# Joining the feature halves of chosen couples on Vector, Silu on Scalar, and expert rows stored by their tile's code

## The reference

```python
# part 2: shared expert and 8 routed experts, the best two per position
shared = silu(x @ Wg_s.T) * (x @ Wu_s.T) @ Wd_s.T
for e in range(8):
    out = out + cw[..., e:e+1] * (silu(x @ Wg[e].T) * (x @ Wu[e].T) @ Wd[e].T)
# part 3: every position against each of 64 text rows
txt_proj = einsum('btd,de->bte', textual, Ws)
feat_proj = einsum('bfd,de->bfe', features, W)
h = tanh(txt_proj[:, None] + feat_proj[:, :, None] + b)     # 512 x 64 x 256 per batch
rho = einsum('bftd,d->bft', h, w[:, 0])
att = softmax(rho + mask)
# part 4: activations scaled, rounded and clipped to +-127, times ternary weights
```

## Time and profile before

| what | us |
|---|---|
| median of 3 runs | 1075.21 (1074.61 to 1077.98) |
| the profiled execution | 1065.32 |
| its span, first to last instruction | 1063.6 |

### The profile page before, as it was taken

One profiled execution on the slowest core, in us unless ns is written; L12 is line 12 of the kernel. 1 busy time (PEld: TensorE's weight loads), 2 busy tenths in 40 slices (PEclk: granted clock), 3 DMA queues, 4 the chain that ended last, 5 costly groups with the idle time before them and its releaser, 6 DMA issues.

```text
span 1063.6 us, 23310 instructions
## 1 busy us (share of the span) xinstructions
PE 975.6 (92%) x8716; PEld 768.0 (72%) x8716; DVE 743.3 (70%) x2077; ACT 655.1 (62%) x900; POOL 216.1 (20%) x260
## 2 busy tenths in 40 slices
PE   5889999999899999999999999999999999966752
PEld 2568888888789999877777777777777777623331
DVE  2757767776634356867577578789578578897996
ACT  1211111211011101799999999899999999899991
POOL 1033312333411122211221221221221121210000
PEclk9869989999899999999999999999999999988986
DMA  8012110111179999766565665664764664100000
GB/s 262 26 65 65 65 40 26 45 40 41 59 252 317 337 344 350 273 222 208 178 212 184 212 221 175 220 222 149 239 223 159 236 215 160 49 21 21 2 21 20
DMA packets 114052, 164.20 MB, mean 154 GB/s; under 512 B 13235, under 2 KB 70068, under 8 KB 113940
## 3 DMA queue, kind: packets, MB, share of 16 engines
q1 hardware_dynamic: 104004, 135.57, 38.3%
q0 software_dynamic: 9936, 27.15, 6.9%
HBM read 138.69 MB, written 23.99 MB: 153 GB/s over the span
## 4 chain that ended last, share of the span: by engine, by line
PE 82%; DVE 8%; issue 6%; POOL 1%; DMA 1%; ACT 1%; SPq 0%; POOLq 0%; DVEq 0%
PE bank L1154 24%; PE bank L1336 18%; PE bank L1315 11%; PE bank L1159 11%; PE bank L1306 5%; PE bank L1323 3%; PE bank L1196 2%; PE bank L1140 2%; PE bank L1268 1%; PE bank L1241 1%; PE bank L1209 1%; PE bank L1229 1%; POOL rows_by_expert L563 1%; DVE arena L1009 1%; PE bank L1362 1%
## 5 line engine op out<-in xcount | busy, mean ns | idle before, releaser
L1154 PEld LDWEIGHTS bank<-rowsT,expert_w 128*128 128x128 f32 x2272 | 269.3, 192 | 21.6 <-issue 17.8
L1154 PE MATMUL bank<-rowsT,expert_w 128*128 128x128 f32 x2272 | 281.1, 277 | 0.5 <-DVE rowsT L955 0.5
L653 ACT ACTIVATE act<-bank 128x512 f32<-128x512 f32 x103 | 60.8, 591 | 204.7 <-PE bank L1154 118.5
L578 POOL DMA_DIRECT2D expert_rows<-rows_out x71 | 42.0, 591 | 455.5 <-DVE rows_out L972 455.5
L1315 PE MATMUL bank<-expert_w,act 128*128 128x256 f32 x568 | 134.5, 380 | 0.0
L1159 PE MATMUL bank<-normT,shared_w 128*128 128x256 f32 x512 | 132.7, 410 | 0.0
L1159 PEld LDWEIGHTS bank<-normT,shared_w 128*128 128x128 f32 x512 | 103.0, 208 | 17.0 <-issue 2.6
L669 ACT ACTIVATE tanhs<-shared_w,txtT 128x512 f32<-128x512 f32 x152 | 108.7, 715 | 4.1 <-DVE shared_w L998 4.1
L1315 PEld LDWEIGHTS bank<-expert_w,act 128*128 128x128 f32 x568 | 102.5, 190 | 11.4 <-issue 0.4
L972 DVE COPY rows_out<-bank 128x256 f32<-128x256 f32 x71 | 30.1, 424 | 112.5 <-PE bank L1315 112.4
L670 ACT ACTIVATE tanhs<-shared_w,txtT 128x512 f32<-128x512 f32 x152 | 108.7, 715 | 0.0
(11 more groups left out here) (233 smaller groups left out, 1467.4 us busy)
## 6 DMA issues: line engine op xcount, KB each, us to landing
expert_w<-in_WgT SPq DMA_DIRECT2D x71, 512.0 KB, 4.2
expert_w<-in_WuT SPq DMA_DIRECT2D x71, 512.0 KB, 5.3
expert_w<-in_WdT SPq DMA_DIRECT2D x71, 512.0 KB, 7.1
rows_in<-rows_by_expert SPq DMA_DIRECT2D x71, 128.0 KB, 5.8
expert_rows<-rows_out POOLq DMA_DIRECT2D x71, 128.0 KB, 4.4
x<-in_x SPq DMA_DIRECT2D x8, 512.0 KB, 4.7
out<-x SPq DMA_DIRECT2D x16, 256.0 KB, 2.2
score<-in_fside SPq DMA_DIRECT2D x8, 128.0 KB, 2.2
```

The source lines that it names most:

```text
L653: e.activation(act[n % 2][:, :], banks[2 * (n % 2)][:, :], ACT.Tanh, scale=0.5).then_inc(s_tanh, 1)
L1154: got = e.matmul(bank[:, i * P:(i + 1) * P], w[:, at:at + P], t[:, c * P:(c + 1) * P], start=c == 0, stop=c == DC - 1)
```

## The change

1. **Couple by couple.** The order in a batch is now couple after couple, both halves of each; a buffer holds a couple. `PAIRS` counts couples out of 32 (it counted groups of two couples out of 16): before 14, 8, 8, 14, 8, 8, 20, 26 couples were pre-added in batches 0 to 7 (106), now 24, 18, 15, 18, 12, 14, 20, 27 (148). Both halves' features are copied at a batch's start.
2. **Join.** For the couples of `JOINS` (16, 5, 12, 6, 17, 12, 1, 0 in batches 0 to 7, 69 in all) one DVE instruction on 128x1024 adds half 0 times `ratio` (the quotient of the two weights of w that meet in a lane) to half 1. PE then sums half 1 alone: 4 products in place of 8. PE waits for the join.
3. **Larger and swap.** So that the quotient is at most 1 in size, each feature of half 0 is exchanged with its partner of half 1 where its weight is the larger: 4 DVE instructions, one product, and 25 more DVE instructions (12 of them 128x256) at the start of the program. The text projection waits for them and comes later on all engines, and so does the conversion.
4. **Silu on ACT** for the 71 routed tiles, with one DVE product after it in place of two instructions. The shared expert keeps the old form. The batches' softmax exp is (1+t)/(1-t) with t = tanh(x/2) in batches 0 to 5 (three more DVE instructions on 128x256 each), and stays Exp in 6 and 7.
5. **Tile's code.** A tile's result is stored in DRAM at its code (POOL reads the code first), and the gather uses the slot numbers of the scatter. The search is gone. `expert_rows` grows to 33792 rows of 1 KB (34.6 MB), and ACT issues one transfer, "blank", that fills it with zeros, in its list after the value copies of the prologue. The first store waits for it.
6. **Rounding** in two DVE instructions in place of four.
7. `AHEAD` is 21: the mix stage starts one tile earlier. The other places and lags are set anew (their tables are shown cut).

```diff
--- before.py
+++ after.py
-AHEAD = 22
+AHEAD = 21
...
-PLACES = {"opened": 25.5, "attend": 72, "route": 36.5, "late": -59, "gather_first": -68, "norm_first": -28, "gather": -1, "norm": 42.5,
-          "mix_in_end": -3, "feature": 20, "sum": 5, "preadd": 3, "mix_out": 9, "mix_out_end": 50}
...
-PAIRS = {0: 7, 1: 4, 2: 4, 3: 7, 4: 4, 5: 4, 6: 10, 7: 13}
+PLACES = {"blank": -62, "opened": 25.5, "attend": 72, "route": 36.5, "late": -59, "gather_first": -68, "norm_first": -15.5,
+          "gather": -2, "norm": 42.5, "mix_in_end": -1, "join": 4.5, "sum": 5, "preadd": 5, "mix_out": 9, "mix_out_end": 50}
...
+PAIRS = {0: 24, 1: 18, 2: 15, 3: 18, 4: 12, 5: 14, 6: 20, 7: 27}
+JOINS = {0: 16, 1: 5, 2: 12, 3: 6, 4: 17, 5: 12, 6: 1, 7: 0}
...
-        pairs, share = self.T // 4, int(PAIRS[b])
-        return m // 2 * share // pairs != (m // 2 + 1) * share // pairs
+        pairs, share = self.T // 2, int(PAIRS[b])
+        return m * share // pairs != (m + 1) * share // pairs
...
+    def joined(self, b, m):
+
+        pairs, share = self.T // 2, int(JOINS[b])
+        return (pairs - 1 - m) * share // pairs != (pairs - m) * share // pairs
...
-        late = [[("text", 0)], [("text", 1)], [("spread",)], [("convert",)]]
+        late = [[("larger",)], [("swap",)], [("text", 0)], [("text", 1)], [("spread",)], [("convert",)]]
...
-        outs_dram = nc.dram_tensor("expert_rows", (RT * P, D), F32, kind="Internal").ap()
+        outs_dram = nc.dram_tensor("expert_rows", ((ABSENT + 8) * P, D), F32, kind="Internal").ap()
...
+                    if r == 0:
+                        e.wait_ge(s_tiles, 1)
+                        e.wait_ge(s_blank, 16)
+                    tile = e.value_load(tile_at[0:1, r:r + 1], min_val=0, max_val=ABSENT + 7)
                     e.wait_ge(s_row_bank, row_no["narrow", n] + 1)
-                    e.dma_start(outs_dram[r * P:(r + 1) * P, :], rows_out[r % OUTS][:, :]).then_inc(s_stored[r % OUTS], 16)
+                    e.dma_start(outs_dram[bass.ds(tile * P, P), :], rows_out[r % OUTS][:, :]).then_inc(s_stored[r % OUTS], 16)
...
+                        out=picked[u % PICKED][:, :], out_offset=None, in_=outs_dram,
+                        in_offset=bass.IndirectOffsetOnAxis(ap=slot_of[j % 2][:, i:i + 1], axis=0)).then_inc(s_picked[u % PICKED], 16)
...
+                elif name == "blank":
+                    e.wait_ge(s_zeros, 1)
+                    e.dma_start(outs_dram.rearrange("(p n k) d -> p n (k d)", p=P, n=BLANKS),
+                                zeros.unsqueeze(1).to_broadcast([P, BLANKS, 1024])).then_inc(s_blank, 16)
...
-                    e.activation(act[n % 2][:, :], banks[2 * (n % 2)][:, :], ACT.Tanh, scale=0.5).then_inc(s_tanh, 1)
+                    if is_routed(n):
+                        e.activation(act[n % 2][:, :], banks[2 * (n % 2)][:, :], ACT.Silu).then_inc(s_tanh, 1)
+                    else:
+                        e.activation(act[n % 2][:, :], banks[2 * (n % 2)][:, :], ACT.Tanh, scale=0.5).then_inc(s_tanh, 1)
...
-                        if m % 2:
-                            e.wait_ge(s_wide_in, wide_in_no[u] + 1)
-                            e.activation(wide_pair[u % WIDE // 2], wide_pair[u % WIDE // 2], ACT.Tanh).then_inc(s_wide, 2)
+                        e.wait_ge(s_wide_in, wide_in_no[b, DC - 1, m] + 1)
+                        e.activation(wide_pair[q % PAIR], wide_pair[q % PAIR], ACT.Tanh).then_inc(s_wide, 1)
...
-                        e.activation(w[:, 0:S], featT[ec], ACT.Tanh, bias=txtT[:, ec, t:t + 1])
-                        e.activation(w[:, S:2 * S], featT[ec], ACT.Tanh, bias=txtT[:, ec, t + 1:t + 2]).then_inc(s_wide, 1)
+                        for ec in range(DC):
+                            for j in range(2):
+                                got = e.activation(tiles[ec][:, S * j:S * (j + 1)], featT[ec], ACT.Tanh, bias=txtT[:, ec, t + j:t + j + 1])
+                        got.then_inc(s_wide, 1)
...
-                    e.activation(rho_e[:, :, :], rho[:, :, :], ACT.Exp).then_inc(s_rho_e, 1)
+                    if b < B - 2:
+                        e.activation(rho_e[:, :, :], rho[:, :, :], ACT.Tanh, scale=0.5).then_inc(s_rho_e, 1)
+                    else:
+                        e.activation(rho_e[:, :, :], rho[:, :, :], ACT.Exp).then_inc(s_rho_e, 1)
...
+                    link(e.tensor_scalar(col_abs, cols[:, WW:WW + DC], -1.0, None, ALU.mult))
+                    chain(lambda: e.tensor_tensor(col_abs, col_abs, cols[:, WW:WW + DC], ALU.max))
+                    chain(lambda: e.tensor_tensor(col_larger, col_abs[:, 0:1], col_abs[:, 1:2], ALU.is_gt))
+                    linked(lambda: e.tensor_scalar(larger_diag, ident[:, :], col_larger, None, ALU.mult)).then_inc(s_larger, 1)
...
+                    e.tensor_copy(larger, bank[:, 0:P]).then_inc(done, 1)
+                    e.wait_ge(s_misc[misc["larger",][0]], misc["larger",][1])
+                    by_col = larger.unsqueeze(1).to_broadcast([P, DC, P])
+                    for weights in (ws, feat_w[:, :, :]):
+                        low, high = weights[:, :, 0:P], weights[:, :, P:D]
+                        chain(lambda: e.tensor_tensor(from_low, low, by_col, ALU.mult))
+                        link(e.tensor_tensor(from_high, high, by_col, ALU.mult))
+                        chain(lambda: e.tensor_tensor(low, low, from_low, ALU.subtract))
+                        link(e.tensor_tensor(high, high, from_high, ALU.subtract))
+                        chain(lambda: e.tensor_tensor(low, low, from_high, ALU.add))
+                        link(e.tensor_tensor(high, high, from_low, ALU.add))
...
+                    chain(lambda: e.tensor_scalar(ratio[:, :], cols[:, WW + 1:WW + 2], 0.0, None, ALU.is_equal))
+                    for c in range(DC):
+                        link(e.tensor_copy(pick_w[:, c, 31:32], cols[:, WW + c:WW + c + 1]))
+                    chain(lambda: e.tensor_tensor(ratio[:, :], ratio[:, :], cols[:, WW + 1:WW + 2], ALU.add))
+                    chain(lambda: e.reciprocal(ratio[:, :], ratio[:, :]))
+                    linked(lambda: e.tensor_tensor(ratio[:, :], ratio[:, :], cols[:, WW:WW + 1], ALU.mult)).then_inc(s_swapped, 1)
...
+                    if is_routed(n):
+                        e.wait_ge(s_up, n + 1)
+                        e.tensor_tensor(h[:, :], h[:, :], bu[:, :], ALU.mult).then_inc(s_h, 1)
+                        continue
                     link(e.scalar_tensor_tensor(out=h[:, :], in0=h[:, :], scalar=1.0, in1=bg[:, :], op0=ALU.add, op1=ALU.mult))
...
-                    if b:
-                        e.wait_ge(s_wide, unit_of(b - 1, ec, T // 2 - 1) + 1)
+                    read = [m for m in range(T // 2) if b and not plan.added(b - 1, m)]
+                    if read:
+                        e.wait_ge(s_wide, pair_of(b - 1, read[-1]) + 1)
+                    if wide_in_no and b and plan.added(b - 1, T // 2 - 1):
+                        e.wait_ge(s_wide_in, wide_in_no[b - 1, DC - 1, T // 2 - 1] + 1)
...
+                elif name == "join":
+                    b, m = k
+                    q = pair_of(b, m)
+                    low, high = halves_of[q % PAIR]
+                    e.wait_ge(s_wide, q + 1)
+                    e.scalar_tensor_tensor(out=high, in0=low, scalar=ratio[:, 0:1], in1=high, op0=ALU.mult, op1=ALU.add).then_inc(s_joined, 1)
...
                     e.wait_ge(s_rho_e, b + 1)
+                    if b < B - 2:
+
+                        link(e.tensor_scalar(rho[:, :, :], rho_e[:, :, :], -1.0, 1.0, ALU.mult, ALU.add))
+                        chain(lambda: e.reciprocal(rho[:, :, :], rho[:, :, :]))
+                        chain(lambda: e.scalar_tensor_tensor(out=rho_e[:, :, :], in0=rho_e[:, :, :], scalar=1.0, in1=rho[:, :, :],
+                                                             op0=ALU.add, op1=ALU.mult))
...
-                    link(e.scalar_tensor_tensor(out=r, in0=r, scalar=inv_step, in1=sm["A"][:, :], op0=ALU.mult, op1=ALU.mult))
+                    link(e.scalar_tensor_tensor(out=r, in0=r, scalar=0.0, in1=sm["S"][:, :], op0=ALU.max, op1=ALU.mult))
...
-                    chain(lambda: e.tensor_scalar(o, v, 0.0, QMAX, ALU.max, ALU.min))
-                    chain(lambda: e.scalar_tensor_tensor(out=v, in0=v, scalar=0.0, in1=o, op0=ALU.min, op1=ALU.add))
-                    chain(lambda: e.tensor_scalar(v, v, -QMAX, ROUND, ALU.max, ALU.add))
-                    linked(lambda: e.tensor_scalar(q, v, -ROUND, None, ALU.add)).then_inc(s_quant, 1)
+                    chain(lambda: e.tensor_scalar(v, v, ROUND, ROUND + QMAX, ALU.add, ALU.min))
+                    linked(lambda: e.tensor_scalar(q, v, ROUND - QMAX, -ROUND, ALU.max, ALU.add)).then_inc(s_quant, 1)
...
-                    b, ec, m = k
-                    u = unit_of(b, ec, m)
-                    if (ec, m) == (0, 0):
+                    b, m = k
+                    q = pair_of(b, m)
+                    if plan.joined(b, m):
```

(11 more changed lines are left out.)

172 lines of the change are left out of this document (93 added, 79 removed).

## The result

The changed kernel takes 1082.28 us, median of 12 runs (1078.8 to 1086.51). The kernel before, run beside it, took 1075.15 (12 runs, 1073.64 to 1080.42). The ratio is 1.0061, with a 95% interval of 1.004 to 1.0081: slower by some 7 us, where 13.5 us faster was forecast.

The account below looks back on a forecast made before the run. PE was taken to bound the mix stage, ACT 3% behind, DVE with room. Mix -14.5, earlier tile -4.3, tail -0.6, table load +1.3, rounding -2.4, start +7.0 gave -13.5: 1075.2 to 1061.7, forecast 1062, range 1045 to 1083 (own 1056 to 1075).

Parts of the forecast that it names:

- the friction of 1 us a batch: Mix stage: waits among three nearly full engines working in order cost 6 us over six batches, between bounds 0 and 20.5.
- PE's load: Mix stage: each join saves PE 8 instructions, 0.45 us; 68 joins save 30.5 us, from batches of 80.0 and 79.8 us.
- DVE's prices: Mix stage: a join takes 1.14 us, a pre-added couple 1.58, the tanh softmax's three instructions about 0.46 each, 1.4 a batch.
- The load of batch 0: First mix batch: DVE rises from 57.3 to 81.5 us and is the bound there; PE 72.8, ACT 71.9.
- The rival "DVE becomes the bound": Mix stage: joins at 1.38 us that each wait a little lose all 20.5 us, giving 1076 or slower; chance 0.18.
- the signs named against the forecast: ACT idle tens of us after 29; PE waits over 15 us; ACT idle for feature copies; joins over 1.4 us.
- The start: Program start: swap work on DVE makes the first scores 4.5 us late, plus 2.5 for the clock: +7.0 us, not given back.
- The 2.5 us for the clock: Program start: PE idles longer, the clock may drop earlier and slow the text and spread products; 2.5 us, bounds 0 and 5.4.
- the blank's issue at 0: Program start: issuing the blank holds ACT 0.4 to 2 us, inside DVE's 4.5 us lateness, so it costs 0.
- the tile earlier: Before the mix stage: one tile fewer, so everything there begins 5.5 us sooner; net -4.3 us.
- the table load: ACT: two new table loads, one where ACT idles, one before batch 6's Exp at 1.28 us: +1.3 us.
- rounding: Closing path: the last batch's rounding loses two of four DVE instructions per half, -2.4 us.

Follow-up runs that it names:

- Exp (7): The changed kernel with the mixing softmax by Exp in all batches instead of the tanh form; ratio 0.9923 to the kernel before, 14.8 us faster than the changed kernel.
- no reciprocal (13): The changed kernel with the 128x256 reciprocal in the mixing softmax left out (weights come out wrong); ratio 0.9965 to the kernel before, 10.3 us faster than the changed kernel.
- fewer pre-adds (8): The changed kernel, all 68 joins, with pre-added couples cut to 18, 11, 8, 10 in batches 0, 2, 4, 5; ratio 0.9936 to the kernel before.
- Experiment 10: The changed kernel without joins and swap, with Exp in the mixing softmax; ratio 0.9971 to the kernel before, against 0.9977 without Exp.
- experiment 3: The changed kernel without joins and without the comparison and swap at the start; ratio 0.9977 to the kernel before, 4.2 us faster than the kernel without joins.
- experiment 4: The changed kernel with the 34.6 MB blank issued later, at 98.4 us; ratio 1.0048 to the kernel before, no difference from the changed kernel that can be told.
- experiment 12: The kernel before, unchanged, for a second trace: the hole ahead of the tiles is there, first tile's matmul at 318.16 us; its median is 1075.7 or 1075.8 on chips with it.

## Why the prediction was wrong

The six batches of the mix stage beside the tiles, from the traces, in us (the number of the experiment in brackets):

| kernel | joins in them | PE busy | PE stands | six batches | DVE busy |
|---|---|---|---|---|---|
| before | 0 | 482.5 | 0.8 | 483.3 | 357.8 |
| no joins (2) | 0 | 484.8 | 0 | 484.8 | 368.8 |
| five a batch (5) | 30 | 474.3 | 5.8 | 480.1 | 402.2 |
| changed (1) | 68 | 463.9 | 25.4 | 489.3 | 444.0 |
| Exp (7) | 68 | 462.7 | 16.7 | 479.4 | 432.6 |
| no reciprocal (13) | 68 | 466.1 | 17.7 | 483.9 | 435.7 |
| fewer pre-adds (8) | 68 | 461.8 | 15.4 | 477.2 | 416.5 |

- **The mix stage, the friction of 1 us a batch.** This is the step that failed. The batch was to take the largest of the three engines' loads plus 1 us, "as PE now stands 0.8 us in 480": 459.5 + 6. It took 489.3. The largest busy times that the trace shows for each batch (83.8 DVE, 76.9, 76.1 and 79.1 PE, 74.8 ACT, 76.0 PE) add up to 466.7, so the friction was 22.6 us, not 6, and PE's waits for DVE alone are 25.3. PE's earlier calm was no evidence: DVE had some 20 us of room a batch then, and the prediction's own count left it none in batch 0 and 0.1 to 2.5 us in batches 2, 4 and 5. The change gives that room to joins and pre-adds that stand in the same queue as the copies for which PE waits. The Exp (7) and the missing reciprocal (13) take 11.4 and 8.3 us from DVE and make the six batches 9.9 and 5.4 us shorter; the fewer pre-adds (8) take 27.5 and give 12.1. Experiment 10 shows no such gain without joins. How much of the 22.6 us is DVE's load and how much only the order in its list is not shown: no run sets the places of joins and copies anew with the same work.
- **PE's load.** This was mis-sized too. The forecast has 448.5 us for PE in the six batches, the trace 463.9. Its windows of 80 us hold 480 us, where the six batches of before are 483.3, and its price of 0.45 us a join was not reached on the whole: against experiment 2 the 68 joins took 20.9 us from PE's busy time, 0.31 each, not 30.5. One reason is seen in the row above, where eight sums after a wait lasted 0.64 us, not 0.45.
- **DVE's prices.** The join was nearly right: 1.19 us from start to start (445.94 to 447.13, duration 1.28, first trace) against 1.14. The tanh form was not: 2.58 us (534.16 to 536.74) against 1.4, nearly all by the reciprocal. An operation that the trace did not show was priced by its shape instead of being bounded. Both prices put right add 3.6 us to the sum of 459.5, so they are the smaller part of the miss. DVE's total was forecast as 433.3 and is 444.0; they are 9.3 of the 10.7 between.
- **The load of batch 0** was nearly right (81.5 forecast, 83.8 busy), and DVE was named as the bound there; its length was not: 89.1, with DVE at 94% and PE standing 7.5 us.
- **The rival "DVE becomes the bound"** had the mechanism ("if joins run at 1.38 and each waits a little, all of the 20.5 us goes ... some friction beyond that is slower"), and a chance of 0.18. Its sum was 1076, though, with joins at 1.38; they ran at 1.19, and the loss came from waits. Of the signs named against the forecast two occurred: PE waited for joins and for L1012 and L1033 11.1 + 2.5 + 1.6 + 0.6 = 15.8 us in total, just over the 15 named; and ACT waited for the next batch's feature copies (L1062), 2.7 us in four places.
- **The start**: +7.0 forecast, +8.0 at the first gate activation; only 3.2 are left at the first tile, but the swap is worth 4.2 us by experiment 3. That it "is not given back" holds for the swap; what brings the first tile forward beside it isn't shown. The 2.5 us for the clock in this sum have the right sign (granted 0.67 instead of 1.00 from 28 to 40 us), but no run prices them.
- **Right:** the first scores at 37.1; the blank's issue at 0, by its 0.64 us on ACT and by experiment 4; the tile earlier (-4.7 for -5.5); the table load (1.28 us at batch 6, though that batch took 2.7 more, of which the softmax of batch 5 is a part: 2.6 less with Exp in 7); rounding (-2.6 for -2.4); batch 7.
- **The drain of a table load**, which the Trainium skill ("ScalarE: Activation LUTs", What ACT_TABLE_LOAD costs) puts at 1.4 us on top of the load: the trace disagrees where it shows a load between two activations. The activation before ended at 530.66, the load starts at 530.68, the Exp at 531.97. The sum needed no more than the 1.3 us.
- **Medians and profile.** The 9.9 us between the profiled execution of before and its median, kept as a constant, are most likely the hole of experiment 12: the second trace of before has it and is 11.7 us longer.

## What to carry to other kernels

Room on an engine is not for sale at its full width when another engine waits for it in order: a bound of "largest load plus a little" held here without joins (DVE at 69 to 79% of a batch, PE standing 0) and nearly with five a batch (78 to 87%, 0 to 1.7 us). In the changed kernel it failed: PE stood 1.3 to 1.7 us at 87% and 4.2 to 7.5 at 91 to 94%. The share alone is no safe sign, as batch 4 of experiment 8 shows, with PE standing 6.5 us at 81% and 17 joins in it; why is not shown. Price a new operation by its own kind, not by its shape, and where no row of it exists, let the bound be wide: one reciprocal made 10 us by experiment 13. When work is moved between engines, choose its amount by a short series: here 30 joins were 6 us faster than none and 11 us faster than 68.

## What the runs showed of the hardware that was not expected

- A reciprocal of 128x256 f32 on DVE takes 1.75 us, where other operations on that shape take 0.28 to 0.43; on 128x4 it takes 0.18.
- The issue of one transfer of 34.6 MB from ACT's queue holds ACT 0.64 us; 1 MB from SP had held SP 1.95. The transfer and the loads beside it moved 415 GB/s from 50 to 75 us, above the 339 of the tiles' stage.
- A hole, in which DVE waits 6.6 to 13.6 us for a releaser that the trace calls remote, ACT stands too and PE has single matmuls while GpSimd issues scatters, is in all seven traces from two chips and in none of the eight from two others, for kernels before and after alike. The kernel before takes 10 us more on the two chips that show it.
